# Products of a VectorE-filled tile of ones in place of TensorE's opening turns of the identity

## What is computed

```python
def cond(x, w, W_base, b_base, As, Bs):
    out = einsum('btc,oc->bto', x, W_base) + b_base
    h = einsum('btc,erc->bter', x, As)
    lora = einsum('bter,eor,be->bto', h, Bs, w)
    return out + lora * 2.0

def ffn(x, gate_w, w_gate, w_up, w_down, sw_gate, sw_up, sw_down):
    scores = softmax(x @ gate_w.T)
    topk_w, topk_i = top_k(scores, 2)            # normalised, times 2.5
    g = silu(einsum('td,edf->etf', x, w_gate)) * einsum('td,edf->etf', x, w_up)
    y = sum over the two experts of topk_w * (g @ w_down)
    return y + silu(x @ sw_gate) * (x @ sw_up) @ sw_down

out = x + ffn(cond(x, ...), ...)
```

## Time and profile before

| | |
|---|---|
| median of 3 runs | 495.78 us (494.04 to 497.9) |
| the profiled execution's own time | 496.81 us |
| its span, first to last instruction | 495.0 us |
| TensorE busy | 486.6 us (98%) |
| VectorE, ScalarE, GpSimd busy | 349.8, 261.8, 220.3 us |
| share of TensorE in the chain that ended last | 93% |

### The profile page before, as it was taken

The page is one execution under the profiler, slowest core; times in us unless marked ns, Lnnn a source line. Parts: engine busy times, 40 slices in busy tenths (PEclk is TensorE's granted clock), DMA queues, the critical chain, the costliest instruction groups (busy, mean ns, idle before and its releaser), DMA issues.

```text
span 495.0 us, 9758 instructions
## 1 busy us (share of the span) xinstructions
PE 486.6 (98%) x3069; PEld 448.7 (91%) x3070; DVE 349.8 (71%) x785; ACT 261.8 (53%) x526; POOL 220.3 (45%) x231
## 2 busy tenths in 40 slices
PE   8999999999999999899999998999999999999997
PEld 7999988888888899899999998999999999888886
DVE  3557866888886556676777766667766776479896
ACT  3577876666562445475555544555555553444322
POOL 2042338564640444565776555565556552211100
PEclk9999999999999999999999999999999999999999
DMA  7497579372222244444444443444444442599942
GB/s 201 153 299 224 172 204 329 118 219 86 44 85 44 86 106 121 116 118 117 127 118 117 117 126 96 122 115 115 127 117 119 117 118 65 154 376 310 384 159 85
DMA packets 104952, 74.53 MB, mean 151 GB/s; under 512 B 61962, under 2 KB 99860, under 8 KB 104916
## 3 DMA queue, kind: packets, MB, share of 16 engines
q1 hardware_dynamic: 97712, 55.20, 38.4%
q0 software_dynamic: 6816, 18.62, 12.6%
q10 hardware_dynamic: 388, 0.27, 0.2%
HBM read 40.25 MB, written 20.32 MB: 122 GB/s over the span
## 4 chain that ended last, share of the span: by engine, by line
PE 93%; DMA 2%; DVE 2%; issue 1%; ACT 1%; SPq 0%; POOL 0%; DVEq 0%; another core or an unknown queue 0%; POOLq 0%
PE bank L286 22%; PE bank L288 22%; PE bank L287 22%; PE bank L831 10%; PE bank L833 5%; PE bank L803 5%; DMA pick<-y_rows 1%; PE bank L596 1%; PE bank L608 1%; PE bank L604 1%; DMA y_rows<-y_sb,dst_i 1%; PE bank L605 1%; PE bank L741 1%; PE bank L740 1%; DVE acc L1432 1%
## 5 line engine op out<-in xcount | busy, mean ns | idle before, releaser
L571 POOL DMA_INDIRECT y_rows<-y_sb,dst_i x71 | 70.0, 985 | 84.1 <-DVE y_sb L1407 83.8
L286 PE MATMUL bank<-w_all,rt_h 128*128 x284 | 97.5, 343 | 0.0
L288 PE MATMUL bank<-w_all,rt_l 128*128 x284 | 91.6, 323 | 0.0
L287 PE MATMUL bank<-w_all,rt_h 128*128 x284 | 91.5, 322 | 0.0
L565 POOL DMA_INDIRECT rows<-x_halves,tok_i x71 | 68.7, 968 | 25.0 <-issue 21.1
L831 PE MATMUL bank<-w_all,gt_h 128*128 (+1 forms) x213 | 78.1, 397 | 0.0
L1001 ACT CAST gt_h<-bank 128x512 fp32r<-128x512 f32 (+1 forms) x47 | 27.5, 585 | 85.7 <-DVE bank L1310 77.1
L286 PE MATMUL bank<-xs_h,sg_h 128*128 128x512 f32 x176 | 70.4, 400 | 0.0
L287 PE MATMUL bank<-xs_l,sg_h 128*128 128x512 f32 x176 | 68.9, 391 | 0.0
L288 PE MATMUL bank<-xs_h,sg_l 128*128 128x512 f32 x176 | 68.7, 390 | 0.0
L1394 DVE TENSOR_TENSOR g<-bank,act 128x352 f32<-128x352 f32 x71 | 37.2, 525 | 42.3 <-issue 33.8
(11 more groups left out here) (192 smaller groups left out, 1114.4 us busy)
## 6 DMA issues: line engine op xcount, KB each, us to landing
pick<-y_rows SPq DMA_DIRECT2D x16, 512.0 KB, 7.8
x_halves<-x_half SPq DMA_DIRECT2D x8, 512.0 KB, 3.3
xin<-in_x_dram SPq DMA_DIRECT2D x7, 512.0 KB, 4.8
w_own<-in_L_ffn_w_gate_dram SPq DMA_DIRECT2D x8, 352.0 KB, 4.2
w_own<-in_L_ffn_w_up_dram SPq DMA_DIRECT2D x8, 352.0 KB, 4.7
y_sb<-in_x_dram SPq DMA_DIRECT2D x5, 512.0 KB, 3.4
base_rows<-y_sb SPq DMA_DIRECT2D x5, 512.0 KB, 2.8
acc<-base_rows SPq DMA_DIRECT2D x5, 512.0 KB, 7.5
```

Source lines behind the costliest of these rows:

```text
L286: pe.matmul(o, lh, rh, start=start, stop=False, skip_group_check=skip)
L287: pe.matmul(o, lh, rl, start=False, stop=False, skip_group_check=skip)
L288: return pe.matmul(o, ll, rh, start=False, stop=stop, skip_group_check=skip)
L571: pool.indirect_dma_start(y_dram, bass.IndirectOffsetOnAxis(ap=dst_i[:, i:i + 1], axis=0), y_sb[:, i % 4, :], None).then_inc(s_sc[i % 4], 16)
```

## The change

VectorE gets a new first instruction, a memset to 1.0 of 128 columns of `act`, which raises a new semaphore `s_warm`. TensorE waits for it in place of `s_ident`, and its opening work is 14 products of that tile with itself (type fp32, 128 x 128 by 128 columns, `matmul` and no longer `transpose`) in place of 12 turns of the identity. The wait for `s_ident` stands behind them, ahead of the turns of `a_raw`.

```diff
-    WARM = 12
+    WARM = 14
...
-        s_xfirst = sem("s_xfirst")
+        s_xfirst, s_warm = sem("s_xfirst"), sem("s_warm")
...
+            pe.wait_ge(s_warm, 1)
+            for _ in range(WARM):
+                pe.matmul(bank[5][:, 0:P], act[:, 0:P], act[:, 0:P], start=True, stop=True)
             pe.wait_ge(s_ident, 1)
-            for _ in range(WARM):
-                pe.transpose(bank[5][:, 0:P], ident[:], ident[:])
...
         @block.vector
         def _(v):
+            v.memset(act[:, 0:P], 1.0).then_inc(s_warm, 1)
             v.wait_ge(s_dcond, 16)
```

## The result

The changed kernel takes 498.11 us (median of 22 runs) where the kernel before, timed beside it, takes 495.05 us: a ratio of 1.0048, 95% interval 1.0024 to 1.0071, which is 2.4 us with 1.2 to 3.5. The ratio is taken over fast executions alone (one can also fall into a slower state) and is not the quotient of the two medians, which lie 3.1 us apart. Timed again later, with the experiments, where both kernels ran more evenly, it is 1.0045 (1.0032 to 1.0058), 2.2 us with 1.6 to 2.9. The profiled execution of the changed kernel took 497.05 us, with a span of 495.1 us.

The account below looks back on a forecast made before the run. TensorE was taken as the bound, its opening delay unhidden: 16 more instructions (3.5 us), less 0.4, 0.7, 0.9 and 0.1, give +1.4 us on the 495.78 us median, so 497.2 us, range 494.7 to 499.5.

Parts of the forecast that it names:

- What bounds it: Whole kernel: TensorE is busy 98% of the span, so time ahead of its first real work is not hidden.
- The early start: Opening: VectorE's memset ends at about 1.04 us, so TensorE starts at 1.1 us, 0.37 us sooner.
- The sum: Opening: 3.5 us for 16 more instructions, less 0.4, 0.7, 0.9 and 0.1; last `xin` turn 1.4 us later.
- The cover of `at_l`: Opening: VectorE's `at_l` ends about 7.9 us, before the condition's turn at 8.0; covered by 0.1 to 0.2 us.
- Two instructions to a product: Opening products, L627: each fp32 product is two instructions, so 14 products are 28 instructions where there were 12.
- The rival of one instruction: Opening products: each is one instruction of 0.22 us, ending at 4.2 us; 495.6 us, chance 8%.
- The price of one: Opening products: an instruction takes 0.11 us at full clock, 0.22 at half; the upper bound is twice that.
- The doubled one: Opening products: an instruction twice as long, 0.43 us cold and 0.22 warm; +4.4 us, 500.2 us, chance 10%.
- Where the clock rises: Opening: TensorE goes from half to full rate at 5.5 to 5.9 us; +1.2 to +1.4 us, chance 55%.
- The rival with an early rise: Opening: products raise the clock sooner than turns; rise at 3.5 us gives +0.2 us, 496.0 us, chance 15%.
- Nothing takes the delay back: After the opening: no later independent wait absorbs the full 1.4 us; the absorbing rival, 495.8 us, had chance 9%.
- The cold rival: Opening: products of ones do not raise the clock, all 28 instructions and ten turns cold; over 500.8 us, chance 3%.

## Why the prediction was right, and what it missed

The direction, the mechanism and the range were right: 497.2 us forecast and 498.11 measured, inside 494.7 to 499.5, slower by a little and by less than 1%. The size was low: +1.4 us forecast and +2.4 (1.2 to 3.5) by the ratio. In order:

- What bounds it. TensorE's time ahead of its real work is paid in full. `tok_i` moved by 0.90, 2.09 and 4.42 us where `xt_h` had moved by 0.90, 2.06 and 4.39.
- The early start. I had 1.1 us and a gain of 0.37; it was 1.12 and 0.35. VectorE's memset took 0.17 us from 0.90. The sum lacked the longer first step of the products, 0.37 us where that of the turns is 0.27.
- The cover of `at_l`. It ended at 7.24 in the first profile, ahead of the turn of the condition at 7.45, so it cost nothing.
- Two instructions to a product. x28, as worked out from x8 for L658. The rival of one instruction is out, and 7 products, which make 14 instructions, cost nothing.
- The price of one. 0.11 at the full and 0.21 at the half rate, the lower bound, which I took. The doubled one is out: loading and streaming of 128 columns overlap in products of fp32 as in turns.
- Where the clock rises. This step failed as it was put. I wrote 5.5 to 5.9 us. In the changed kernel it was 4.4 to 4.6 in three profiles and 7.0 to 7.1 in two, and in the other variants with opening work from 5.3 to 7.4. No opening of the changed kernel had the rise that I wrote. The sum with one value came out at 1.4 and the mean over five openings is 1.35, but that is luck: it hangs on how many early and late rises fell among the five. The rival with an early rise had a chance of 15%; three profiles of five lie between its 3.5 us and my 5.5, and its time, 496.0 us, was not measured.
- Nothing takes the delay back. True up to 161 us in the profiles, and the ratios show a loss at the end.
- The cold rival. Products of ones were followed by the rise each time, but in two of five openings only at 7.0 to 7.1 us, so that all 28 instructions were cold, as this rival had it; the ten turns behind them were not.

What is left over is the gap between the opening's 1.35 us and the 2.2 to 2.4 us of the ratios. The intervals begin at 1.2 and 1.6 us, so the first holds it, and the forecast's 1.4, and the second does not. Among the experiments, the four spans of the changed kernel are 492.6, 493.2, 493.4 and 492.3 us and the two of before 490.5 and 490.8: 2.2 us on average, of which 1.5 are in these openings (`xt_h` at 7.71 on average against 6.24). The other 0.7 us arises after 161 us and differs from profile to profile: in two of the four the scatter of the last blocks and the loads of the sums are in the chain (5.1 us and 6.1 to 6.4 us), in one a gather at 214 us, in one nothing of the kind. This is one of the first two:

```profile
422.10 5.10 DMA y_rows<-y_sb,dst_i
428.33 6.10 DMA pick<-y_rows
```

The profile of the kernel with 7 products, which has the same program behind its opening, shows none of this (its span is 490.9), and its time is that of before. With 12 products of the identity, which has neither the memset nor the new wait, the same pieces are in the chain (5.1 and 6.2 us), so the memset and the new wait are not needed for them. Nor is a longer opening: they stand in the chain of the first profile of before, and in that of the 28 products of bf16 (5.2 and 6.3 us), whose `xt_h` is as early as in the kernel before and whose span is 492.5 us. Whether the later phase makes them more frequent, or it is chance in a few profiles, stays open. The time with 28 products is also above its profile (6.6 us against 4.4), whose execution was the fastest of the four. A later rise in the others could do that only if it came near 10 us (2.2 us at 0.48 for each microsecond, on top of 5.35), and with opening work none was seen after 7.4, so this excess stays open too.

No variant beat the kernel before. The best of them, with 7 products or 6, cannot be told from it.

## To carry to other kernels

In this kernel, work that only keeps TensorE busy was free as long as it ended when the first real operand landed. Size it in executed instructions and their time at the half rate, not in statements: a product of fp32 is two instructions where a transpose is one, and a product of bf16 is one of half the length. Starting it a few tenths sooner bought nothing here, while every instruction past the landing cost 0.11 us or 0.21 us, and the cost was still there at 161 us and in the whole time. Leaving it out altogether cost 3.4 us.

## What the runs showed of the hardware that I had not expected

- The profile's clock column cannot be used ahead of its first change: without opening work it reads 1.00 from 4.4 us on, and the steps of 0.22 us say half rate until 13.3 us. Steps between starts of equal instructions tell it.
- Without the opening work the rise took 8.9 us from TensorE's first instruction, though TensorE was busy for 3.98 of the 4.00 us from 4.4 to 8.4, with turns and then narrow products; with it, 3.2 to 5.9 us in the kernels above. The rise moved by 2.7 us between executions of the changed kernel, and by 0.01 us between three of the kernel before.
- After an early rise the clock fell back to 0.50 from 8.7 to 12.1 us in one profile, with no wait longer than 0.62 us ahead of it and TensorE busy for 2.68 of the 3.3 us before. The Trainium skill, TensorE: Matmul & The Clock Gate, section Why this matters for your kernels, says that drops in mid-kernel are avoided by leaving no idle gaps of a few microseconds between bursts of matmuls. There was no such gap here, and the clock fell all the same.
